# Edge stage of a graph network: GpSimd makes a quarter of the messages of each step's fourth tile, from a ScalarE copy of its weights

## The reference

```python
for W in (W_mlp1, W_mlp2, W_mlp3):
    h = SILU_2MOM * jax.nn.silu(h @ W / jnp.sqrt(jnp.float32(W.shape[0])))
tpw = h @ W_mlp4 / jnp.sqrt(jnp.float32(W_mlp4.shape[0]))
w1, w2, w3, w4 = jnp.split(tpw, 4, axis=-1)
s0 = x0[sender]
s1 = x1[sender]
p1 = w1 * s0 * y0
p2 = (w2 * s0)[:, :, None] * y1[:, None, :]
p3 = w3[:, :, None] * s1 * y0[:, None, :]
p4 = w4 * jnp.einsum('eum,em->eu', s1, y1) / SQRT3
m0 = jnp.concatenate([p1, p4], axis=-1)
m1 = jnp.concatenate([p2, p3], axis=1)
msg0 = jax.ops.segment_sum(m0, receiver, num_segments=num_nodes)
msg1 = jax.ops.segment_sum(m1, receiver, num_segments=num_nodes)
```

## Time and profile before

| what | value |
|---|---|
| median of 3 runs | 1586.83 us (1585.8 to 1586.88) |
| the profiled execution | 1584.67 us |
| its span in the trace | 1582.6 us |
| TensorE busy in the span | 90% |
| VectorE busy in the span | 90% |
| ScalarE busy in the span | 71% |
| GpSimd busy in the span | 60% |
| first message operation, last `close` ends | 899.69 us, 1431.92 us |

### The profile page before, as it was taken

The page is one execution under the profiler, slowest core; times in us unless marked ns, Lnnn a source line. Parts: engine busy times, 40 slices in busy tenths (PEclk is TensorE's granted clock), DMA queues, the critical chain, the costliest instruction groups (busy, mean ns, idle before and its releaser), DMA issues. The chain is left out here.

```text
span 1582.6 us, 26974 instructions
## 1 busy us (share of the span) xinstructions
PE 1429.9 (90%) x9070; PEld 948.4 (60%) x9070; DVE 1424.8 (90%) x1808; ACT 1123.7 (71%) x2530; POOL 954.2 (60%) x761
## 2 busy tenths in 40 slices
PE   5848999999999999999996698889889898886998
PEld 3536788888888888888884433333333333335787
DVE  7888999999999999999999699999999999993555
ACT  6356888888888888888885677777777777762343
POOL 4155788888888888888803366666666666652000
PEclk9878999999999999999998799999999999997999
DMA  9356363636262626272122488888888888874231
GB/s 344 133 221 185 78 210 69 219 64 224 58 230 50 238 43 245 36 253 29 21 72 85 166 276 257 268 259 269 260 267 264 260 266 265 257 250 160 92 107 53
DMA packets 88560, 281.02 MB, mean 178 GB/s; under 512 B 23770, under 2 KB 26004, under 8 KB 81899
## 3 DMA queue, kind: packets, MB, share of 16 engines
q1 hardware_dynamic: 42776, 166.90, 28.4%
q0 software_dynamic: 45648, 112.41, 27.3%
HBM read 379.98 MB, written 78.21 MB: 290 GB/s over the span
## 5 line engine op out<-in xcount | busy, mean ns | idle before, releaser
L802 DVE TENSOR_TENSOR weights_hl<-arena,weights_hl 128x1024 fp32r<-128x1024 f32 x486 | 578.0, 1227 | 38.2 <-ACT weights_hl L1098 36.7
L1647 POOL DMA_INDIRECT sorted_edges<-arena x320 | 502.6, 1571 | 103.8 <-issue 90.2
L1098 ACT ACTIVATE weights_hl<-arena 128x1024 fp32r<-128x1024 f32 x486 | 500.3, 1060 | 70.2 <-PE pair L1397 70.2
L1678 POOL DMA_INDIRECT arena<-node_table,arena x352 | 337.1, 958 | 219.8 <-DVE arena L912 102.2
L1397 PE MATMUL pair<-weights_hl,rows_hl 128*128 128x512 f32 x1944 | 463.9, 396 | 4.4 <-ACT weights_hl L1098 2.2
L1397 PEld LDWEIGHTS pair<-weights_hl,rows_hl 128*128 128x128 f32 x1944 | 358.1, 189 | 94.7 <-DVE weights_hl L802 16.9
L912 DVE TENSOR_TENSOR arena<-pair,arena 128x768 f32<-128x768 f32 x352 | 317.1, 937 | 0.0
L1216 ACT ACTIVATE arena<-arena 128x32 f32<-128x32 f32 x1408 | 313.2, 311 | 2.7 <-DVE arena L893 2.6
L1497 PE MATMUL pair<-arena 64*128 64x512 f32 x704 | 195.6, 630 | 57.1 <-DVE arena L912 56.2
L1397 PE MATMUL pair<-weights_hl,hidden_hl 128*128 128x512 f32 x972 | 236.7, 397 | 0.0
L1397 PEld LDWEIGHTS pair<-weights_hl,hidden_hl 128*128 128x128 f32 x972 | 177.8, 188 | 37.1
(11 more groups left out here) (254 smaller groups left out, 1295.6 us busy)
## 6 DMA issues: line engine op xcount, KB each, us to landing
arena<-in_w SPq DMA_DIRECT2D x81, 2048.0 KB
arena<-in_w SPq DMA_DIRECT2D x81, 1024.0 KB
sums<-arena SPq DMA_DIRECT2D x88, 512.0 KB, 4.3
arena<-in_v SPq DMA_DIRECT2D x16, 512.0 KB, 4.5
pair_rows<-arena SPq DMA_DIRECT2D x1, 6966.0 KB, 29.3
arena<-pair_rows SPq DMA_DIRECT2D x27, 256.0 KB, 3.3
arena<-node_table,arena POOLq DMA_INDIRECT x352, 4.3
sorted_edges<-arena POOLq DMA_INDIRECT x320
```

What stands on the lines that cost most here:

```text
L802: v.tensor_tensor(out=part[s][:, 1], in0=by_chunk(n)[4], in1=part[s][:, 0].bitcast(F32), op=ALU.subtract).then_inc(v_low, 1)
L1098: a.activation(out=part[s][:, 0], in_=cols, func=ACT.Copy).then_inc(a_high, 1)
L1647: g.indirect_dma_start(out=sorted_edges, out_offset=bass.IndirectOffsetOnAxis(ap=slot_i[:, j:j + 1], axis=0), in_=er[:, j, :], in_offset=N ...
L1678: g.indirect_dma_start(out=row, out_offset=None, in_=table, in_offset=bass.IndirectOffsetOnAxis(ap=senders[:, i:i + 1], axis=0)).then_inc( ...
```

## The change

`messages_of(s, 1)` leaves w1 and w2 times s0 of the second tile of its pair (tile 3 of the step) out: its first operation is 128x256 now, not 128x512. ScalarE copies these 256 weights from PSUM to SBUF (`copy_weights`, at the start of each step's work, two buffers `w_copy`), and GpSimd multiplies the copy by the gathered row (`products_of`, between the second and the third gather that it issues in a step). Two semaphores are new: `a_wcopy` (the copy is made) and `g_msg` (the product is made). VectorE waits for `a_wcopy` ahead of the last operation of each step, because the `v_msg` that this one raises also tells TensorE that the bank is free. `sum_up`, the gather into the buffer that the product read, and the copy two steps later wait for `g_msg`. The number of gathers, picks and matrix products is the same. After it, lines are numbered anew: L910 and L917 for L907 and L912, L1705 for L1678, L1229 for the copy and L1694 for the product.

```diff
+        w_copy = phase_tensors(edge_weights0=(2 * MUL, F32), edge_weights1=(2 * MUL, F32))
@@ messages_of
-                v.tensor_tensor(out=m[:, :, 0:2],
-                                in0=tp[:, :].rearrange("p (t w u) -> p t w u", t=2, w=4)[:, :, 0:2],
-                                in1=rows_in[:, :, 0:1].to_broadcast([128, 2, 2, MUL]), op=ALU.mult)
+                n = 2 - h
+                v.tensor_tensor(out=m[:, 0:n, 0:2],
+                                in0=tp[:, :].rearrange("p (t w u) -> p t w u", t=2, w=4)[:, 0:n, 0:2],
+                                in1=rows_in[:, 0:n, 0:1].to_broadcast([128, n, 2, MUL]), op=ALU.mult)
                 for t in range(2):
+                    if h and t:
+                        v.wait_ge(a_wcopy, s + 1)
@@ scalar
+            def copy_weights(s):
+                a.wait_ge(p_tp, (s + 1) * Q)
+                if s >= 2:
+                    a.wait_ge(g_msg, s - 1)
+                a.activation(out=w_copy[s % 2], in_=tp_bank[Q - 1][:, 0:2 * MUL], func=ACT.Copy).then_inc(a_wcopy, 1)
             for s, gap in enumerate(mlp_gaps):
+                copy_weights(s)
@@ sum_up
                 pe.wait_ge(v_msg, (s + 1) * Q)
+                pe.wait_ge(g_msg, s + 1)
@@ gpsimd
+            def products_of(s):
+
+                i = s * Q + Q - 1
+                g.wait_ge(a_wcopy, s + 1)
+                g.wait_ge(d_gat[i % NGAT], 16 * (i // NGAT + 1))
+                if s >= 2:
+                    g.wait_ge(p_sum, s - 1)
+                g.tensor_tensor(out=msg_pair[s % 2 * 2 + 1][:, 1, 0:2],
+                                in0=w_copy[s % 2].rearrange("p (w u) -> p w u", w=2),
+                                in1=gat_pair[i % NGAT // 2][:, 1, 0:1].to_broadcast([128, 2, MUL]), op=ALU.mult
+                                ).then_inc(g_msg, 1)
@@ gather
                     g.wait_ge(v_msg, i - NGAT + 1)
+                    if i % Q == Q - 1:
+                        g.wait_ge(g_msg, (i - NGAT) // Q + 1)
@@ the loop over steps
                     if i < NTILE:
                         gather(i)
+                    if i % Q == 1 and s < STEPS:
+                        products_of(s)
```

More of the change, by code:

```diff
@@ L356, in program @@
         a_pick, a_mlp = sem("picks_made"), sem("mlp_activated")
+        a_wcopy, g_msg = sem("edge_weights_copied"), sem("fourth_tile_products")
         p_prod, p_tp, p_sum = sem("mlp_product"), sem("edge_weights"), sem("step_summed")
```

## The result

| | median | runs | ratio to the kernel before, 95% interval |
|---|---|---|---|
| before | 1586.32 us | 1582.82 to 1586.88 | |
| after | 1564.60 us | 1562.89 to 1565.88 | 0.9867 (0.9856 to 0.9879) |

The change makes the kernel 1.33% faster, by 21.7 us between the medians. The forecast was 1565.4. The profiled execution took 1564.73 us, its span is 1562.6.

A forecast was written before the change was run, and what follows sets the result against it. VectorE's own work was taken to bound the edge stage, at 6.00 us a step. A gain of 22.9 us less 1.5 lost at the start gave -21.4 us, so 1565.4 us, with an 8-in-10 range of 1562 to 1583.

The forecast's parts named there:

- The bound and VectorE's term: Edge stage: VectorE sets the pace; its step falls from 6.00 to 5.74 us, 22.9 us over 88 steps.
- ScalarE's copy at nothing: Edge stage: the 0.39 us copy lies in ScalarE's idle time with 2.9 us of slack, so costs nothing.
- GpSimd's product: Edge stage: product takes 0.60 us of 0.70 left; GpSimd's step of 5.64 us stays under 5.74.
- Rival A: Edge stage: GpSimd becomes the bound but some gain is left, for products of 0.70 to 0.96 us; chance 0.20.
- The start: Start of edge stage: late tenth gather delays VectorE's third step, costing 0 to 3 us, taken as 1.5.
- Rival B: Edge stage: GpSimd and VectorE shut each other out, making the kernel slower, such as 1618.5 us; chance 0.14.
- Rival C: Edge stage: waits for ScalarE's copy or GpSimd's product eat the gain, leaving 1587 us; chance 0.06.

The follow-up runs named there:

- e6: The changed kernel with ScalarE's copy made three times a step, two into buffers nobody reads; 1562.70 us, ratio 0.9864 to the kernel before.
- e3: The changed kernel with GpSimd's product made twice, the second into a buffer nobody reads; 1605.48 us, ratio 1.0126 to the kernel before.
- e4: The changed kernel with the change beginning only at the fifth step, VectorE making all earlier products; 1564.03 us, ratio 0.9868 to the kernel before.
- a1: The changed kernel run again unaltered, as yardstick for its group; 1564.36 us, ratio 0.9871 to the kernel before.
- e1: The changed kernel without copy, product and their waits, VectorE's operation still shortened; 1564.09 us, ratio 0.9869 to the kernel before.
- e2: The kernel before with copy, product (into an unread buffer) and waits added, VectorE still making all messages; 1584.33 us, ratio 0.9990 to the kernel before.
- e7: The changed kernel with GpSimd also making the third tile's product every eighth step, in one 128x512 product; 1567.43 us, ratio 0.9889 to the kernel before.
- e9: The changed kernel with GpSimd also making the third tile's product every eighth step, as two 128x256 instructions; 1570.11 us, ratio 0.9908 to the kernel before.
- e8: The changed kernel with GpSimd also making the third tile's product every second step, in one 128x512 product; 1596.29 us, ratio 1.0065 to the kernel before.
- e5: The changed kernel with VectorE's every-fourth-step table moved behind the step's last message operation, beside GpSimd's product; 1566.03 us, ratio 0.9879 to the kernel before.

## Why the prediction was right, and where it wasn't

**The bound and VectorE's term: right.** 0.26 us a step was forecast. The steps without a table went from 5.85 to 5.58 us, 0.27 less; with all that delays some steps, the average fell by 0.256 us in the profiled execution and by 0.22 to 0.24 in the three later ones. The shrunk operation is 0.33 us from start to start and 0.40 long, 0.35 and 0.40 expected. The wait ahead of the last operation shows no idle time. It has a second use that I had not named: without it ScalarE's copy and VectorE's last operation could read one PSUM bank at the same time; what that would do, no run shows.

**ScalarE's copy at nothing: right.** 379 ns where 0.39 us was put, and e6 makes it three times for free.

**GpSimd's product: right side, two sizes off.** It takes 0.65 us where I took 0.60. But its net cost is 0.52, since the next gather starts 0.16 us after it, not 0.30, of the 0.70 us that it had to spend. One error takes back part of the other: the step came out at 5.57, forecast 5.64. That 0.60 was near was in part luck, since it was put together from one-input operations of other kinds. By the Trainium skill's 2.6 cycles an element for two inputs (GPSIMD Engine Reference, section 3.1) an estimated 0.56 us had been worked out for the product; the measured 0.65 us is above it. Rival A did not come about in the change. e3, whose products take 1.11 us, more than the 0.96 where A's gain ends, fits its sum within 5 us.

**The start: the term that had the wrong cause.** I allowed 1.5 us for a tenth gather that lands too late for VectorE's third step. In none of the four traces of the changed kernel does that step wait for a gather: it waits 0.40 us for TensorE's weights, as it did before (0.39). A late product is no better cause: e4 has no product at the start and waits 2.1 us in its first `close`; a1 has it and waits 0.6. What goes with that wait is when TensorE's clock rises. But a loss of about that size came from elsewhere. Later in the stage VectorE's first operation of a step waits now and then, put down to a gather or to no event: 0.1, 2.0, 0.8 and 1.6 us in all in the four traces of the change, 1.0 in e1, none in the kernel before. The median from issue to landing is 5.3 us now, 4.3 before. The stretched tables are the other part (0.7 us in the profiled execution). With the term at 0 the forecast would have been 1563.9. The runs don't tell that from 1565.4, and that 1565.4 lies so near to the measured 1564.6 is partly luck.

**Rival B: refuted for the messages, confirmed for the table.** In the profiled change VectorE's messages keep their 937 ns, and e2 adds the product at no cost that shows. The table with its two SBUF inputs is stretched to 1.08 us from 0.68 when a product has begun just before it; when the table begins first, the product is stretched, and in some cases both are (0.86 and 1.06 us in the change). The prediction put the table "some 4 us ahead of the product's turn" and overlooked the product of the step before, which ends only 0.9 us ahead of it. So the change has some of these meetings itself, for 0.7 us in its profiled execution; e7 and e9 show what comes of it when GpSimd falls behind and meets most of the tables.

**Rival C: refuted** by e1 and e6.

## What to carry to other kernels

When one engine is busy all the time, the gain from relieving it is the distance from start to start that it gives up, and the question is only whether the helper's step, gaps of its indirect DMAs included, stays below the new one; the busy share (64% here) says nothing of that, the distances (5.04 of 6.00 us) do. Put a helper's work where the next instruction of its own queue doesn't wait for it, and away from VectorE operations that read two SBUF inputs, on both sides of them. A helper that is brought near its limit drifts in phase, and then meets what it had been kept away from.

## What the runs showed of the hardware that I had not expected

- A GpSimd product of 128x256 float32 out of SBUF takes 0.65 us (0.59 from start to start behind another, e3), one of 128x512 takes 1.10 (e8). An indirect DMA starts 0.16 us after it, but 0.30 after another indirect DMA.
- A GpSimd indirect DMA that waits for the semaphore of the GpSimd product right ahead of it starts 0.75 us after the product's end (61 times in e7, e8 and e9), where one that doesn't starts after 0.16. That the wait is the cause is inferred.
- A VectorE product with two SBUF inputs that starts while a GpSimd one runs is longer: 1.08 us, not 0.68 (e5). When the VectorE one starts first, the product takes 1.10 us (e5), and in some cases both are longer (1.09 and 1.08 us, e9). A VectorE operation with an input from PSUM keeps its 0.94 (e5).
- At the start of the stage TensorE's clock rose from its lower level 7.8 us after the first message operation in a1 and 11.3 us after it in e4, and the first `close` waited 0.6 us and 2.1 us.
